# Four pairs of products are added by accumulating transfers instead of on TensorE

## What is computed

```python
xdw = depthwise_3x3(x) + dw_b
om = xdw @ om_w + om_b              # for each of 32 groups: 9 offsets (y, x) and 9 masks
value = x @ vp_w + vp_b             # 32 groups of 8 channels
sampled = bilinear(value, pixel + tap + offset)          # 9 taps
out = sum over taps of sampled * mask
return out @ op_w
```

## Time and profile before

| | |
|---|---|
| median of 3 runs | 3881.9 us (3876.7 to 3891.0) |
| profiled execution, its time | 3880.1 us |
| its span | 3878.3 us |
| layer 0, its 32 steps | from 94 us to about 3410 us |
| one step | 101 to 105 us |
| TensorE busy, share of the span | 94% |
| VectorE busy | 91% |
| ScalarE busy | 59% |
| DMA, software queue (GpSimd) and hardware queue (SP), share of 16 engines | 28.2% and 23.0% |

### The profile page before, as it was taken

How to read it: one execution, slowest core, us unless ns; L and a number is a source line. 1 busy time by engine, 2 the same in 40 slices (tenths; PEclk the granted TensorE clock), 3 DMA queues, 4 the chain that set the end, 5 groups by cost and what they waited for, 6 DMA issues and landing times. The chain is left out here.

```text
span 3878.3 us, 90671 instructions
## 1 busy us (share of the span) xinstructions
PE 3634.4 (94%) x37696; PEld 2370.7 (61%) x37696; DVE 3511.8 (91%) x2757; ACT 2286.1 (59%) x4547; POOL 565.0 (15%) x412
## 2 busy tenths in 40 slices
PE   3799999999999999999999999999999999858998
PEld 1466666666666666666666666666666666623333
DVE  2799999999999999999999999989999999958776
ACT  3665666666556656666666666665566665325554
POOL 0011100111111111111110111111111111104444
PEclk9999999999999999999999999999999999979999
DMA  5454555556554455456545555555545544335563
GB/s 142 109 118 100 116 112 121 111 109 121 131 121 100 96 124 122 101 110 132 129 98 115 117 124 119 109 113 126 117 98 107 105 103 94 60 147 201 214 215 146
DMA packets 319939, 470.35 MB, mean 121 GB/s; under 512 B 37244, under 2 KB 242684, under 8 KB 313736
## 3 DMA queue, kind: packets, MB, share of 16 engines
q0 software_dynamic: 94080, 196.11, 28.2%
q1 hardware_dynamic: 224872, 266.08, 23.0%
q10 hardware_dynamic: 544, 2.10, 0.1%
HBM read 262.53 MB, written 67.41 MB: 85 GB/s over the span
## 5 line engine op out<-in xcount | busy, mean ns | idle before, releaser
L984 DVE TENSOR_TENSOR pv<-val,wsum 128x2048 f32<-128x2048 f32 x800 | 1812.5, 2288 | 7.4 <-PE ps_add L791 7.4
L791 PEld LDWEIGHTS ps_add<-ident,pv 128*128 128x128 f32 x12800 | 1403.0, 142 | 350.0 <-issue 237.2
L791 PE MATMUL ps_add<-ident,pv 128*128 128x128 f32 x12800 | 1529.5, 276 | 65.4 <-DVE pv L984 57.1
L746 PE MATMUL ps_om<-xdw,omw 128*32 128x256 f32 x13824 | 872.0, 385 | 26.9 <-ACT hat L585 26.0
L937 DVE TENSOR_TENSOR prod<-hat,mwy 128x1536 f32<-128x1536 f32 (+1 forms) x384 | 526.5, 1399 | 96.5 <-DMA wsum<-prod 75.5
L474 POOL DMA_DIRECT2D wsum<-prod x192 | 226.0, 1254 | 2598.9 <-DVE wsum L937 2598.9
L583 ACT ACTIVATE hat<-ps_om,omb 128x256 f32<-128x256 f32 x576 | 276.1, 479 | 552.1 <-PE ps_om L746 506.8
L746 PEld LDWEIGHTS ps_om<-xdw,omw 128*32 128x32 f32 x13824 | 391.8, 110 | 328.6 <-issue 95.9
L587 ACT ACTIVATE msk<-ps_om,omb 128x256 f32<-128x256 f32 x288 | 137.1, 476 | 401.6 <-PE ps_om L746 399.4
L923 DVE TENSOR_TENSOR mwy<-hat,msk 128x768 f32<-128x768 f32 x288 | 275.0, 955 | 93.8 <-ACT hat L597 93.8
L718 PE MATMUL ps_bg<-tri,diag 128*32 128x512 f32 x3024 | 347.3, 593 | 0.0
(11 more groups left out here) (120 smaller groups left out, 2607.8 us busy)
## 6 DMA issues: line engine op xcount, KB each, us to landing
wsum<-prod POOLq DMA_DIRECT2D x160, 768.0 KB, 7.0
tri<-in_x_dram SPq DMA_DIRECT2D x725, 128.0 KB, 2.9
win<-in_x_dram SPq DMA_DIRECT2D x148, 256.0 KB, 3.5
x<-xres SPq DMA_DIRECT2D x128, 256.0 KB, 5.2
xres<-in_x_dram POOLq DMA_DIRECT2D x124, 256.0 KB, 8.7
out_dram<-c_x SPq DMA_DIRECT2D x31, 1024.0 KB, 4.7
c_x<-x SPq DMA_DIRECT2D x30, 1024.0 KB, 5.4
c_box<-box_d SPq DMA_DIRECT2D x16, 1024.0 KB, 7.1
```

Of the source, the lines that this page charges most:

```text
L746: mm = nc.tensor.matmul(ps_om[G * q:G * q + G, (par + i) % 2, 0:TOK], omw[:, h, comp, :], xdw[:, j % 2, h, q, :], start=h == 0, stop=h == ...
L791: mm = nc.tensor.matmul(ps_add[:, tb, c, :], pv[:, (j + uv) % PBUF, c, P * tb:P * tb + P], consts["ident"][:, :], start=uv == 0 and c % 4 ...
L984: nc.vector.tensor_tensor(pv[:, (j + uv) % PBUF, :, :].rearrange("p c (r w) -> p c r w", w=W), val[:, :, SR * j + u:SR * j + u + SR, v:v + ...
```

## The change

Shifts 1, 3, 12 and 15 get a partner: 0, 2, 11 and 14 (`PAIRED`). Once VectorE has written product uv of such a pair, GpSimd issues an accumulating transfer, from the partner's buffer of `pv` to that of uv (1 MB), under a new semaphore `pair_added`. TensorE then adds only uv, after that transfer, and not the partner: 21 products in place of 25. `multiply` waits for `pair_added` where the buffer that it takes was read by a transfer (shifts 4, 6, 15, 18), and else for `add_done` as before. The order of the adds changes: `ADDS_AT` puts 1 at k = 5, 3 at k = 6 behind 4, 12 at k = 0 behind 13, 15 at k = 1 behind 16. A paired add always comes in the late part of its tap.

```diff
+PAIRED = {1: 0, 3: 2, 12: 11, 15: 14}
+PAIRS = list(PAIRED)
+ADDS_AT = [(13, 12), (16, 15, 17, 18), (19, 20, 21), (22, 23, 24), (), (1,), (4, 3, 5, 6), (7, 8, 9), (10,)]
+ADDED = [uv for k in (4, 5, 6, 7, 8, 0, 1, 2, 3) for uv in ADDS_AT[k]]
+ADDS = len(ADDED)
...
+                def add_pair(n, j, uv):
+
+                    s = STEPS * n + j
+                    pool.wait_ge(pv_full, SHIFTS * s + uv + 1)
+                    at_least(pool, pair_added, 16 * (len(PAIRS) * s + PAIRS.index(uv)))
+                    nc.gpsimd.dma_start(pv[:, (j + uv) % PBUF, :, :], pv[:, (j + PAIRED[uv]) % PBUF, :, :], accum_op=ALU.add)\
+                        .then_inc(pair_added, 16)
+
                 for n in range(NI):
                     for j in range(STEPS):
+                        if (n, j) != (0, 0):
+                            add_pair(*previous(n, j), 15)
                         for k in SENT_TAPS:
-                            if k == 6 and j < CH and n < NI - 1:
-                                load_ahead(n, j, 0, "back3")
+                            if k == 6:
+                                if j < CH and n < NI - 1:
+                                    load_ahead(n, j, 0, "back3")
+                                add_pair(n, j, 1)
+                                add_pair(n, j, 3)
                             add_products(n, j, k)
                         if j < CH and n < NI - 1:
                             load_ahead(n, j, 1, "project3")
                         if (n, j) != (0, 0):
                             add_residual(*previous(n, j), unit(n, j, "project3", NI) + 1)
+                        add_pair(n, j, 12)
+                add_pair(NI - 1, STEPS - 1, 15)
...
-                    act.wait_ge(add_done, SHIFTS * (s + 1))
+                    act.wait_ge(add_done, ADDS * (s + 1))
...
                 def add(s, j, uv):
-                    pe.wait_ge(pv_full, SHIFTS * s + uv + 1)
-                    if uv == 0:
+                    if uv in PAIRED:
+                        pe.wait_ge(pair_added, 16 * (len(PAIRS) * s + PAIRS.index(uv) + 1))
+                    else:
+                        pe.wait_ge(pv_full, SHIFTS * s + uv + 1)
+                    if uv == ADDED[0]:
                         at_least(pe, add_out, s)
...
-                                                  consts["ident"][:, :], start=uv == 0 and c % 4 == 0,
-                                                  stop=uv == SHIFTS - 1, is_transpose=True, skip_group_check=True)
+                                                  consts["ident"][:, :], start=uv == ADDED[0] and c % 4 == 0,
+                                                  stop=uv == ADDED[-1], is_transpose=True, skip_group_check=True)
...
-                    def add_next(k, i):
-                        if k < SAMPLED and not first:
-                            add(s - 1, j - 1, SAMPLES_AT[k][i])
-                        elif k >= SAMPLED and i < len(SAMPLES_AT[k]):
-                            add(s, j, SAMPLES_AT[k][i])
+                    def add_next(k, early):
+
+                        before = [uv for uv in ADDS_AT[k][:1] if uv not in PAIRED]
+                        for uv in before if early else ADDS_AT[k][len(before):]:
+                            if k >= SAMPLED:
+                                add(s, j, uv)
+                            elif not first:
+                                add(s - 1, j - 1, uv)
...
-                        add_next(k, 0)
+                        add_next(k, True)
...
-                        add_next(k, 1)
-                        add_next(k, 2)
+                        add_next(k, False)
...
-                    if not isinstance(s, int) or s > 0 or uv >= PBUF:
-                        dve.wait_ge(add_done, SHIFTS * s + uv - PBUF + 1)
+                    used, in_step = (uv - PBUF, s) if uv >= PBUF else (uv - PBUF + SHIFTS, s - 1)
+                    if used in PAIRED.values():
+                        dve.wait_ge(pair_added, 16 * (len(PAIRS) * in_step + list(PAIRED.values()).index(used) + 1))
+                    elif not isinstance(s, int) or in_step >= 0:
+                        dve.wait_ge(add_done, ADDS * in_step + ADDED.index(used) + 1)
```

More of the change, by code:

```diff
@@ L292, in layer0 @@
         pv_full, add_done, add_out = sem("pv_full"), sem("add_done"), sem("add_out")
+        pair_added = sem("pair_added")
         xres_added, stats2 = sem("xres_added"), sem("stats2")
@@ L850, in _ @@
                 for k in range(SAMPLED):
-                    for uv in SAMPLES_AT[k]:
+                    for uv in ADDS_AT[k]:
                         add(STEPS * NI - 1, STEPS - 1, uv)
```

## The result

The changed kernel takes 4098.8 us (median of 4 runs, 4091.5 to 4100.4) against 3883.2 us before: ratio 1.055 (95% interval 1.053 to 1.057), 215 us slower. The forecast was 4060 us, 3935 to 4150. The profiled execution took 4099.8 us, so its rows stand for the median.

The account below looks back on a forecast made before the run. VectorE's own chain was taken to set the pace, TensorE close behind. New waits 77 + 52 + 60 + 39 = 228, less 47 of relief, gave +181 us on 3880.1: 4060 us, range 3935 to 4150 (8 in 10).

Parts of the forecast that it names:

- What bounds the kernel: Whole kernel: VectorE's own chain sets the pace, TensorE follows close behind; lighter TensorE gives back at most 47 us.
- these 47 us: VectorE's idle time hanging on TensorE, 40.2 us before mask rows and 7.1 before multiplies; all taken as gain, -47 us.
- One pair, 8.4 us: An accumulating 1 MB transfer lands in 8.4 us: 6.9 for a tap's 768 KB plus 1.5; bounds 5.2 and 9.6.
- Rival 1: Pairs land soon enough that shift 15 and tap 7's products never wait; TensorE's relief shows: 3833 us, chance 10%.
- Rival 3: In between: a pair lands in 6.8 us, waits of 104 less 47 give +57, 3937 us; chance 15%.
- Pair 12, +77: Before shift 15: pair lands in 10.2 us beside the window, has 7.8; wait 2.4 us in 32 steps, +77 us.
- Pair 15, nothing: Before shift 18: 10.2 us against 8.4 needed, and tap 1's transfer behind the pair in time; costed at nothing.
- Pair 3 and tap 6: Tap 6's transfer queues behind the pair; tap 7's products wait 2.9 us in 18 steps without load ahead: +52 us.
- Pair 1 and the load ahead: Steps 0 and 1: pair queued behind the load delays shift 4 through tap 7: 8.6 and 5.6 us, +60 and +39.
- The late adds, nothing: Adds of 1, 3, 12 and 15 come later, and shifts 5, 7, 16 and 19 need their buffers; costed at nothing.
- The second rival: Buffers held by late adds: shift 7 waits about 1.9 us each step for add 3, +61, 4120 us; chance 15%.
- clock as now: TensorE's granted clock in layer 0 was to stay as before the change, where the stretch showed 0.99.

Follow-up runs that it names:

- relief_ordered: Kernel before, no transfers of products, TensorE never adds shifts 0, 2, 11 and 14, shifts 1 and 3 kept in late slots: 3853 us, ratio 0.993.
- only_pair12: Kernel before with only shift 11 going to 12 by a transfer, the other adds TensorE's: 3950 us, ratio 1.018.
- only_pair3: Kernel before with only shift 2 going to 3 by a transfer, the other adds TensorE's: 3927 us, ratio 1.012.
- load_behind: Changed kernel with the load ahead of steps 0 and 1 put behind pairs 1 and 3 and tap 6's transfer on GpSimd's queue: 4026.7 us, ratio 1.037.
- after_filled: Changed kernel with the first offsets of each tap computed twice, making TensorE as busy as before: 4155 us, ratio 1.071.

## Why the prediction was right or wrong

**What bounds the kernel: right.** relief_ordered takes 4 of TensorE's 25 adds away and gains 26 us of 243. That TensorE "gives back at most these 47 us" holds; that it gives all of them was too much. With nothing else changed 11 us came back as waits for taps; inside the changed kernel the masks' waits fell by 41 us, and some 13 of these came back before tap 8. That TensorE "should no longer be late" was right for the hats and wrong for the adds.

**One pair, 8.4 us: near for the median, too long for a pair alone.** The 8.2 us (6.9 to 13.2) are a median over pairs many of which have other transfers beside or ahead of them. Pair 3, which has the engines to itself in most steps, lands in 7.1 us at the median, in the changed kernel and alone, where the sum of the earlier trace rows and a third more bytes gave 8.4. Rival 1, and with it the rule of the Trainium skill (DMA: Bandwidth & Descriptors, Anatomy of one DMA), needed about 6 or less; the trace disagrees with the 4.4 us that this rule gives by estimate, for no pair landed in under 6.9 us. Rival 3's 6.8 us is nearer to the measured 7.1 than the forecast's own 8.4; its time, 3937, fails by the terms that neither sum had.

**Pair 12, +77: wrong in size.** I took 8.4 us for the pair and, from the earlier trace rows, 1.8 more for 1 MB on SP's queue, as the window goes out at the same moment. It lands in 8.5 us (median, only_pair12), not in 10.2. Most of the error is the 8.4: against the 7.1 of pair 3 the window adds some 1.4 us. The term is 21 us in the changed kernel and 31 alone.

**Pair 15, nothing: wrong.** The failed step is "Tap 1's transfer comes behind the pair in the queue, but its products are made only at 1649 to 1652 and the pair's service ends near 1647 + 7". These numbers speak against the nothing: the pair's service then ends at 1654, tap 1's 4.4 us of service follow it, and with the 2.5 us that its 6.9 are longer than its service it lands at some 1660.9, 1.6 us after tap 2's products want to start. By this estimate the term was some 50 us. Measured, tap 1's transfer takes 10.6 us behind a pair that went out 4.9 us earlier, and the term is +48 us. Nearly half of it is in step 3, where only the four statistics stand between.

**Pair 3 and tap 6: right** in mechanism; only_pair3 shows it alone, at 2.0 us a step where I had 2.9, because the pair lands in 7.1 us and not in 8.4.

**Pair 1 and the load ahead: right in mechanism**, as load_behind shows (4027 against 4025, which I expected from the trace of the changed kernel), and mis-sized by step. The steps' mean lengths, counted between the large products of k = 0 from the second image to the seventh, are 105.0, 103.5, 104.2 and 101.7 us before and 111.8, 114.9, 106.8 and 108.5 after; the forecast was 113, 110 and twice 107. In step 1 I let the load go out 1.9 us earlier, since TensorE has an add fewer ahead of it. It goes no earlier: 695.08 is 64 us behind the start of its step (631.05), where the load in the earlier trace rows was 62 us behind its own; why is open. So pair 1 is 2.2 to 6.6 us late in step 1 where I had 0.2. In step 0 the load does go out earlier (62 to 63 us behind the start of the step, 64 before), and pair 1 is 1.9 to 3.8 us late where I had 3.8.

**The late adds, nothing: wrong by 26 us.** The second rival priced this mechanism at shift 7, with 61 us; in the changed kernel it stands at shifts 5, 16 and 19 (2 us at shift 7). The fill of after_filled shows what keeps it small: without "7.6 us more air" the waits for adds are 120 us.

Two misses, 56 us too much at shift 15 and 74 us too little at tap 2 and the late adds, cancelled for the most part; what is left of them and the 20 us at tap 8, which the sum did not have, make most of the 39 us between forecast and measurement. The range held the time for a right reason (VectorE's waits on transfers), and the centre was close partly by luck.

## What to carry to other kernels

Before work is taken off an engine, sum the idle time of the *other* engines that hangs on it; here 47 us for 243 us of work, and 26 were had. A transfer has a price even when it is itself in time: look for the next one behind it on the same queue, and ask how late that may be. Where an in-order engine waits for a transfer, what matters is what stands behind that wait: an order with one or two adds in an earlier slot made the kernel slower twice, by 1.0% with the pair (3912 against 3872 us) and by 1.5% in the relief alone (3910 against 3853 us).

## What I had not expected of the hardware

TensorE's add of 16 transposes takes 1.94 to 1.97 us, but 3.68 us right behind an idle time of 5.4 us, and 3.42 us behind one of 4.5. It is no single case: 36 of the changed kernel's 672 adds come right behind an idle time of more than 4 us and take 3.1 to 3.7 us, where the kernel before had one such. Two stretches of the changed kernel, first the one around the first of them:

```profile
708.00:714.00 6.00, 5.12 (x44) 4.20 (x48) 4.57 (x3) 0.30 (x1) 2.07 (x2) 0.61 0.56 109
714.00:726.00 12.00, 12.00 (x100) 8.87 (x90) 7.33 (x6) 5.00 (x12) 1.16 (x2) 1.00 0.52 100
```

The granted clock is 0.61 in the first and 1.00 in the second: after it stood idle TensorE works at the lower of its two levels (1.2 of 2.4 GHz) for a part of the first. Over the run 0.948 were granted, 0.984 before. By estimate, 3.68 less 1.97, an add that waited for a transfer can then cost VectorE up to 1.7 us more, if its buffer is the next one needed. The prediction had said "clock as now"; that was wrong, and no run here isolates what it costs.
